# The order of TensorE's instructions: each transpose alone between two large matmuls

## What is computed

```
q = int8_linear(layernorm(x), wq, bq)          # rows quantised to 8 bits
k = cond @ wk.T + bk;  v = cond @ wv.T + bv    # float32
attn = softmax(q k^T / sqrt(32) + mask)        # 16 heads of 32
x = x + int8_linear(attn @ v, wo, bo)
h = layernorm(x)
probs = softmax(h @ router.T); two best of 8 experts a token, weights normalised
x = x + sum over the two of w * (silu(h @ gate) * (h @ up)) @ down
```

## Time and profile before

| | us |
|---|---|
| median of three runs | 1616.57 (1613.74 to 1618.61) |
| the profiled execution | 1616.73 |
| its span, first to last instruction | 1615.0 |
| one item in the middle of `attention`, from its first score (616.50) to the next item's (649.07) | 32.57 |
| TensorE busy | 1501.2 (93%) |
| VectorE, ScalarE, GpSimd busy | 899.4, 881.5, 660.9 |

### The profile page before, as it was taken

How to read it: one execution, slowest core, us unless ns; L and a number is a source line. 1 busy time by engine, 2 the same in 40 slices (tenths; PEclk the granted TensorE clock), 3 DMA queues, 4 the chain that set the end, 5 groups by cost and what they waited for, 6 DMA issues and landing times. The chain is left out here.

```text
span 1615.0 us, 40110 instructions
## 1 busy us (share of the span) xinstructions
PE 1501.2 (93%) x11594; PEld 1310.1 (81%) x11595; DVE 899.4 (56%) x2365; ACT 881.5 (55%) x2097; POOL 660.9 (41%) x671
## 2 busy tenths in 40 slices
PE   2899999999999999999999999983399999999896
PEld 2778888888888888888888888872299999999895
DVE  6557666766676667666776667654722222222221
ACT  2467667676767676676667667761033333333232
POOL 4233334333343234333333343323555555656453
PEclk9999999999999999999999999996599999999998
DMA  5567777677767776777677767763537766666643
GB/s 175 143 168 194 209 204 193 180 224 207 188 177 222 203 194 179 212 201 205 181 199 208 207 183 189 198 168 129 171 67 186 186 155 144 150 152 127 157 78 48
DMA packets 220125, 281.09 MB, mean 174 GB/s; under 512 B 83569, under 2 KB 164977, under 8 KB 220081
## 3 DMA queue, kind: packets, MB, share of 16 engines
q1 hardware_dynamic: 203952, 247.24, 54.4%
q0 software_dynamic: 16128, 33.30, 11.8%
HBM read 118.31 MB, written 66.17 MB: 114 GB/s over the span
## 5 line engine op out<-in xcount | busy, mean ns | idle before, releaser
L465 DVE CUSTOM_DVE_ANT_0 probs<-score,neg_mask 112x375 f32<-112x375 f32 x512 | 279.9, 547 | 262.2 <-PE score L555 260.7
L393 ACT ACTIVATE probs<-probs,neg_max 112x375 f32<-112x375 f32 x512 | 312.2, 610 | 185.8 <-DVE neg_max L465 183.3
L386 ACT ACTIVATE probs_t<-turn 125x336 f32<-125x336 f32 x512 | 225.0, 440 | 110.1 <-PE turn L563 110.1
L563 PE MATMUL turn<-ident,probs 112*125 112x112 f32 x1536 | 265.0, 281 | 2.9 <-ACT probs L393 2.9
L563 PEld LDWEIGHTS turn<-ident,probs 112*125 112x125 f32 x1536 | 222.7, 188 | 38.0 <-issue 14.1
L555 PE MATMUL score<-k_stack,q_stack 96*112 96x376 f32 x512 | 208.4, 407 | 5.9 <-DMA q_stack<-q_lo 5.5
L590 PE MATMUL proj<-ctx_hi,wk_hi 128*128 128x376 f32 x512 | 175.6, 343 | 1.9 <-PEq L29 1.1
L590 PE MATMUL proj<-ctx_hi,wk_lo 128*128 128x376 f32 x512 | 171.9, 336 | 0.0
L590 PE MATMUL proj<-ctx_lo,wk_hi 128*128 128x376 f32 x512 | 171.9, 336 | 0.0
L1031 DVE TENSOR_TENSOR a_lo<-a_ps,a_hi 128x384 fp32r<-128x384 f32 x63 | 35.1, 558 | 244.4 <-ACT a_hi L1006 244.4
L595 PE MATMUL proj<-wv_lo,ctx_hi 128*125 128x512 f32 x384 | 151.7, 395 | 0.0
(11 more groups left out here) (198 smaller groups left out, 3419.9 us busy)
## 6 DMA issues: line engine op xcount, KB each, us to landing
k_stack<-k_hi SPq DMA_DIRECT2D x512, 94.0 KB, 2.2
k_stack<-k_lo SPq DMA_DIRECT2D x256, 94.0 KB, 2.3
ctx_stage<-ctx_t SPq DMA_DIRECT2D x32, 750.0 KB, 5.3
q_stack<-q_hi SPq DMA_DIRECT2D x256, 56.0 KB, 2.0
w_raw<-gate_up_t SPq DMA_DIRECT2D x32, 352.0 KB, 3.1
gate_up_dram_hi<-w_hi SPq DMA_DIRECT2D x32, 352.0 KB, 5.5
gate_up_dram_lo<-w_lo SPq DMA_DIRECT2D x32, 352.0 KB, 5.9
gate_up_hi<-gate_up_dram_hi SPq DMA_DIRECT2D x16, 704.0 KB, 4.9
```

The costliest lines, as they stand in the source:

```text
L386: act.activation(probs_t[:, h % RING_T, :, :], turn[h % 2][0:LC, 0:LT * N].rearrange("p (l n) -> p l n", l=LT), ACT.Copy).then_inc(turned_ ...
L393: act.activation(probs[:, h % DS, :], probs[:, h % DS, :], ACT.Exp, bias=neg_max[:, par % 2, h:h + 1], scale=-1.0, accum_out=total[:, par ...
L465: dve.tensor_tensor_reduce(probs[:, h % DS, :], score[h % 2][0:N, 0:L], neg_mask[:, p, :], 1.0, BIG, ALU.add, ALU.min, neg_max[:, p, h:h + ...
L563: mm = pe.transpose(turn[h % 2][0:LC, l * N:(l + 1) * N], probs[:, h % DS, l * LC:(l + 1) * LC], W["ident"][0:N, 0:N])
```

## The change

Only TensorE's program changes. The same matmuls and transposes are issued with the same waits, in another order. In `attention`, `project` now takes single matmuls instead of threes; the table `FIRST` says with which of the 84 each head begins. In each head the three transposes of probabilities come with one projection matmul behind each, then the score, then the rest of the head's share. Where a head has four small transposes, a projection matmul stands behind each where the share allows (heads 4, 6, 9, 11 and the first of 13; the router's matmuls in head 5 likewise). In head 15 the output matmuls stand between the transposes. In `experts` six gate and up matmuls come first, then each of the seven transposes with one of them behind it, then the other eleven. In the code below, lines taken away in the branches of the heads are left out.

```diff
+    FIRST = [0, 5, 10, 15, 20, 27, 33, 40, 45, 50, 57, 62, 69, 73, 79, 84, 84]
+    assert FIRST[H] == 3 * KT * UNITS
...
-            def turn_probs(b, h):
+            def turn_probs(b, h, l):
                 k = b * H + h
-                need(pe, softmaxed, k + 1)
-                need(pe, turned_out, k - 1)
-                for l in range(LT):
-                    mm = pe.transpose(turn[h % 2][0:LC, l * N:(l + 1) * N], probs[:, h % DS, l * LC:(l + 1) * LC],
-                                      W["ident"][0:N, 0:N])
-                mm.then_inc(turned, 1)
+                if l == 0:
+                    need(pe, softmaxed, k + 1)
+                    need(pe, turned_out, k - 1)
+                mm = pe.transpose(turn[h % 2][0:LC, l * N:(l + 1) * N], probs[:, h % DS, l * LC:(l + 1) * LC],
+                                  W["ident"][0:N, 0:N])
+                if l == LT - 1:
+                    mm.then_inc(turned, 1)
...
+            def project(n, q, h, i, j=None):
+
+                for step in range(FIRST[h] + i, FIRST[h + 1] if j is None else FIRST[h] + j):
+                    u, t, part = step // (3 * KT), step // 3 % KT, step % 3
+                    first, final = t == 0 and part == 0, t == KT - 1 and part == 2
+                    if u == 0 and first:
+                        need(pe, c_lo_made, n + 1)
+                        need(pe, c_hi_made, n + 1)
+                    if first:
+                        need(pe, unit_out, UNITS * n + u - 1)
+                    bank = proj[(q + u) % 2]
+                    if u < KT:
+                        w, c = (("wk_hi", c_hi), ("wk_hi", c_lo), ("wk_lo", c_hi))[part]
+                        mm = pe.matmul(bank[:, 0:LP], W[w][:, t, 128 * u:128 * u + 128], c[:, q, t, :], start=first, stop=final)
+                    else:
+                        l = u - KT
+                        w, c = (("wv_hi", c_hi), ("wv_lo", c_hi), ("wv_hi", c_lo))[part]
+                        mm = pe.matmul(bank[0:LC, :], c[:, q, t, l * LC:(l + 1) * LC], W[w][:, t, :], start=first, stop=final)
+                    if final:
+                        mm.then_inc(unit_made, 1)
+
+            def turn_to_misc(src, ident, dst, t, rows, cols):
+                return pe.transpose(dst[0:cols, t * rows:(t + 1) * rows], src[:, 128 * t:128 * t + 128], ident)
...
                 for h in range(H):
-                    if h < 2 and has_m:
-                        turn_probs(m, H - 2 + h)
-                    if h >= 2 and has_a:
-                        turn_probs(it, h - 2)
+                    for l in range(LT):
+                        if h < 2 and has_m:
+                            turn_probs(m, H - 2 + h, l)
+                        if h >= 2 and has_a:
+                            turn_probs(it, h - 2, l)
+                        if has_n and h < H - 1:
+                            project(n, q, h, l, l + 1)
+                        if h == H - 1 and has_m:
+                            if l == 0:
+                                need(pe, o_out, 3 * m + 2)
+                            pe.matmul(misc[0:N, :], o_int_t[:, l, :], W["wo_int"][:, l, :], start=(l == 0), stop=False)
                     if has_a:
                         scores(it, par, h)
-                    if h < H - 1 and has_n:
-                        for step in range(KT * UNITS * h // (H - 1), KT * UNITS * (h + 1) // (H - 1)):
-                            project(n, q, step // KT, step % KT)
+                    if h == 4:
+                        if has_n:
+                            project(n, q, h, 3, 4)
                         for t in range(KT):
+                            if has_m2:
+                                if t == 0:
+                                    need(pe, ln2, 3 * m2 + 3)
+                                    need(pe, o_out, 3 * m2 + 3)
+                                mm = turn_to_misc(h2_s, W["ident"][0:N, 0:N], misc, t, N, 128)
+                                if t == KT - 1:
+                                    mm.then_inc(r_made, 1)
+                            if has_n and t < KT - 1:
+                                project(n, q, h, 4 + t, 5 + t)
+                    elif h == 5:
+                        if has_n:
+                            project(n, q, h, 3, 4)
+                        for t in range(KT):
+                            if has_m2:
+                                if t == 0:
+                                    need(pe, r_out, 2 * m2 + 1)
+                                mm = pe.matmul(misc[0:N, 0:8], h2_t[:, t, :], W["router"][:, t, :], start=(t == 0), stop=(t == KT - 1))
+                                if t == KT - 1:
+                                    mm.then_inc(r_made, 1)
+                            if has_n and t < 2:
+                                project(n, q, h, 4 + t, 5 + t)
+                    elif h == 6 and has_n:
+                        for t in range(KT):
+                            if t == 0:
+                                need(pe, ln1, 8 * n + 8)
+                                need(pe, q_out, 3 * n)
+                                if has_m2:
+                                    need(pe, r_out, 2 * m2 + 2)
+                            mm = turn_to_misc(x_int, W["ident16"][0:N, 0:N], misc16, t, N, 128)
+                            if t == KT - 1:
+                                mm.then_inc(q_made, 1)
+                            project(n, q, h, 3 + t, 4 + t)
+                    elif h == 7 and has_n:
                         need(pe, q_out, 3 * n + 1)
                         for t in range(KT):
                             mm = pe.matmul(misc[0:N, :], x_int_t[:, t, :], W["wq_int"][:, t, :], start=(t == 0), stop=(t == KT - 1))
                         mm.then_inc(q_made, 1)
+                        project(n, q, h, 3)
+                    elif h == 9 and has_n:
+                        project(n, q, h, 3, 4)
+                        for t in range(KT):
+                            if t == 0:
+                                need(pe, q_biased, n + 1)
+                            mm = turn_to_misc(q_tok, W["ident"][0:N, 0:N], misc, t, N, 128)
+                            if t == KT - 1:
+                                mm.then_inc(q_made, 1)
+                            else:
+                                project(n, q, h, 4 + t, 5 + t)
+                    elif h == 11:
+                        for t in range(KT):
+                            if has_m:
+                                if t == 0:
+                                    need(pe, out_t_out, m + 1)
+                                    if has_n:
+                                        need(pe, q_out, 3 * n + 3)
+                                    if has_m2:
+                                        need(pe, r_out, 2 * m2 + 2)
+                                mm = pe.transpose(misc[0:N, 128 * t:128 * t + 128], out_ts[:, t, :], W["ident"][:, :])
+                                if t == KT - 1:
+                                    mm.then_inc(o_made, 1)
+                            if has_n:
+                                project(n, q, h, 3 + t, 4 + t)
+                    elif h == 13:
                         if has_n:
+                            project(n, q, h, 3, 5)
                         for t in range(KT):
+                            if has_m:
+                                if t == 0:
+                                    need(pe, o_steps, 6 * m + 6)
+                                mm = turn_to_misc(o_int, W["ident16"][0:N, 0:N], misc16, t, N, 128)
+                                if t == KT - 1:
+                                    mm.then_inc(o_made, 1)
+                            if has_n and t == 0:
+                                project(n, q, h, 5, 6)
+                    elif h == H - 1:
+                        if has_m:
+                            pe.matmul(misc[0:N, :], o_int_t[:, KT - 1, :], W["wo_int"][:, KT - 1, :], start=False, stop=True).then_inc(o_made, 1)
+                    elif has_n:
+                        project(n, q, h, 3)
                     if h == 2 and has_m:
                         values(m, par + 1, G4 - 1)
...
+    AHEAD = 6
...
-            def gate_and_up(t, par, place, steps):
-                for k in steps:
-                    for h, w in ((h_hi, "gate_up_hi"), (h_hi, "gate_up_lo"), (h_lo, "gate_up_hi")):
-                        for i, ps in enumerate((gate_ps[par], up_ps[par])):
-                            mm = pe.matmul(ps[:, 0:F], h[:, par, 128 * k:128 * k + 128],
-                                           R[w][:, bass.ds(place * (KT * F2) + (k * F2 + i * F), F)],
-                                           start=(k == 0 and h is h_hi and w == "gate_up_hi"), stop=(k == KT - 1 and h is h_lo))
+            def gate_and_up(t, par, place, first, final):
+                for step in range(first, final):
+                    k, part, i = step // 6, step // 2 % 3, step % 2
```

(36 more changed lines are left out.)

## The result

The changed kernel takes 1704.96 us in the median (1699.43 to 1706.67) against 1616.74 us before (1613.74 to 1618.61, four executions): a ratio of 1.054, 95% interval 1.051 to 1.057. The forecast was 1711 us, slower. The profiled executions stand at 1699.43 us (span 1697.7) and 1616.73 us (span 1615.0), +82.7 us.

The account below looks back on a forecast made before the run. TensorE's instruction list, 93% busy, was taken to bound the kernel. List +0.6 and waits +2.45 us over 31 items, less 2 at the ends, plus 1.5 for experts, gave +94: 1711 us, range 1630 to 1735.

Parts of the forecast that it names:

- (a): Rival, 5%: weight loads run two ahead once spread, a transpose costs 0.05 us; +0.5 us an item, 1634 us.
- (b): Rival, 6%: loads run two ahead and a transpose costs only 0.03 us; -0.65 us an item, some 1596 us, faster.
- The list: TensorE's instructions in an item, start to start without the longer waits: +0.6 us an item, bounds -0.4 and +1.4.
- 16-bit transposes: Four of x_int and one of o_int, put ahead of 32-bit projections, lose their fast loads: +0.3 us an item.
- The waits: TensorE waits longer for chains starting at a score, now behind three projections: +2.45 us an item, bounds 0 and 3.0.
- q_tok, head 9: TensorE waits for the chain from head 8's score through VectorE and GpSimd before transposing q_tok: +1.15 us an item.
- o_int, head 13: TensorE waits for the output chain from head 11's score before transposing o_int: +0.6 us an item.
- key unit 0, head 4: A projection's load waits for the bank that k_lo frees, after head 3's score: +0.45 us an item.
- softmax of head 15, head 1: Head 15's probability transposes, standing in head 1, wait for its softmax: +0.3 us an item.
- (c): Rival, 9%: the waits don't come, since VectorE and GpSimd run earlier than the score; list alone, 1637 us.
- (d): Rival, 4%: neither waits nor a longer list, the spread costs nothing; time within 0.3%.
- (e): Rival, 4%: changing between a transpose and a projection costs 0.09 us; +2.5 us an item more, 1790 us.

Follow-up runs that it names:

- e1: The changed kernel with each head's three probability transposes in a row again, then three projections, then the score in its late place: 1700.8 us, ratio 1.053.
- e5: The kernel before with the new order in the experts stage alone: 1616.8 us, ratio 1.0018.
- e10: The changed kernel with the score ahead of the pairs, q_tok's transposes behind head 9's projections, 16-bit transposes in a row: 1620.2 us, ratio 1.0029.
- e6: The kernel before with only x_int's four 16-bit transposes dealt out among head 6's projections: 1625.2 us, ratio 1.0068.

## Why the prediction was right

**What a transpose costs.** Right. Predicted was 0.112 us ahead of a projection; the pairs give 0.285 - 0.172 = 0.113 on keys and 0.344 - 0.232 = 0.112 on values. Loads run one ahead, spread or not. Rivals (a) and (b) needed pairs of 0.22 us or less on keys and fell with that. The Trainium skill (TensorE: Matmul & The Clock Gate, Engine queue depths) has a queue of 64 that pulls loads ahead of matmuls in flight, and doesn't say how far; no row here shows more than one load ahead.

**The list**, predicted +0.6 us an item. The difference of the items less that of the waits gives 2.87 - 2.14 = 0.73. By the medians of the distances in before and after it is made up so:

| term | predicted | found |
|---|---|---|
| 45 transposes of probabilities | +0.2 | +0.26 |
| 16-bit transposes | +0.3 | +0.37 (x_int 0.30, o_int 0.07) |
| 32-bit transposes on misc, the router | +0.1 | +0.15 (h2_s 0.06, q_tok 0.05, router 0.03, out_ts 0.01) |
| output matmuls between transposes | -0.03 | -0.02 |
| sum | +0.6 | +0.76 |

The sum agrees with 0.73 within the rounding. Each positive term was a little too small. The largest error is the 16-bit transposes: one of x_int ahead of a projection costs 0.13 (pairs of 0.300 less 0.172), where the prediction took 0.11.

**The waits**, predicted +2.45 us an item, by distances in the traces:

| wait | predicted | before | after | difference |
|---|---|---|---|---|
| q_tok, head 9 | +1.15 | 0.16 | 1.17 | +1.01 |
| o_int, head 13 | +0.6 | 0 | 0.55 | +0.55 |
| key unit 0, head 4 | +0.45 | 0.03 | 0.41 | +0.38 |
| softmax of head 15, head 1 | +0.3 | 0 | 0.27 | +0.27 |
| units 1 and 3 | -0.05 | 0.07 | 0 | -0.07 |
| sum | +2.45 | 0.26 | 2.40 | +2.14 |

All four stood where they were said to be, behind the instruction that was named. Rivals (c) and (d) (they don't come) fell by their rows, and rival (e) (a price of the change-over) by e1. Each was predicted a little too large. For two of them the rows show why: I had kept the length of the chain as a constant, from the start of a score that stands behind transposes in before and behind a projection in after. From the score of head 8 to q_tok's load it is 3.28 us before and 3.18 after, to key unit 0's load 2.21 and 2.15.

**Experts**: +1.5 predicted, +1.3 by the tile's period.

**The sum.** 2.87 an item was measured for 3.05 predicted. The waits were 0.31 too large and the list 0.13 too small, so the errors cancel in part, which is luck. Times 31 that is 89, and I had taken 2 off for the ends; measured are 81.5 from the first score to that of the last item. The first four items are the reason for 6.6 of the missing 7.5. Their differences are +1.2, -0.2, +2.8 and +1.1 us: item 0 has no output chain and no softmax of an earlier item to wait for, in item 1 the load engine of before stands idle for 2.6 us ahead of q_tok already, and in item 3 for 1.8 us ahead of a score. In part this is this one profile: e5, whose `attention` is that of before, takes 130.0 us for these four items and before 132.6. This term of the sum was mis-sized. The two errors, 5.6 us on the items and 5.5 at the ends, have the same sign and make the profiled execution 1699.4 for 1711. The median is closer, 1705.0, since this profiled execution is the fastest of its kernel.

**What stays open.** The new dealing of the projections was not run alone, why a 16-bit transpose ahead of a projection costs 0.13 where a 32-bit one costs 0.11 isn't shown, and the first four items differ by 2.6 us between two profiles with the same `attention`.

## What to carry to other kernels

Ahead of any reordering, list the chains that leave the engine and return to it, and add up for each what the engine has to do between its source and its wait: work moved ahead of a source is cover lost, to the full, once the chain's slack is gone. Put the source early in its group and the wait late. Dealing small instructions out among large ones saved nothing here, where only one weight load runs ahead (e1, e10), and where the small ones had fast loads it cost the difference (e6).

## What the runs showed of the hardware that I had not expected

- The start recorded for a projection behind a transpose comes 0.03 to 0.04 us after the transpose's, and the next start is 0.26 later where the rule is 0.17 (e6: 627.37 to 627.63). So the transpose's cost shows up in the distance behind the projection. Only whole pairs can be read, not single distances.
- Ahead of the small matmuls of the values an additional 0.09 us passes (after: 670.92 to 671.26 is 0.34, where a projection behind a 16-bit transpose has 0.26), and before had as much: its last x_int transpose was followed by the values at 0.14 in place of 0.05. It is a price of that border, whatever stands ahead of it, and I have no cause for it.
- A stage total can mislead. Once in the experts TensorE waits for what SyncE has queued: 5.3 us in the profile of before, 3.3 in after, 1.2 in e5. Over all profiles it is 3.5 to 5.5 us with the old order of the experts (five kernels) and 1.2 to 6.6 with the new one (seven), so it has nothing to do with the change. In before the granted clock then fell: TensorE had been idle from 1516.8 us, and from 1519 to 1523 us the mean is 0.54, so mostly the lower level (1.2 GHz). By stage totals (from the first transpose into h_ps to the start of the last down matmul) the new order of the experts would have gained 4.7 us in e5 (432.6 for 437.3), by the tile's period it costs 1.3.
